# Layer-norm tiles and matmuls interleaved, longer leads, and W2 in pieces: a transformer layer on eight cores

## The chip, the cores and the metric

The kernel runs on all 8 NeuronCores of one Trainium2 chip. Every core gets 2 of the 16 sequences and all the weights, and the cores exchange nothing. The metric is the time of one execution on the device, in microseconds (us), taken from the slowest core. Engines in the rows: PE is TensorE (PEld its weight loads), DVE is VectorE, ACT is ScalarE, POOL is GpSimd, SP is SyncE, which here only issues transfers; SPq and POOLq are the issuing queues.

## What is computed

For each sequence of 2048 tokens and width 1024, one pre-norm layer with 16 heads of 64:

```python
x = x + proj(softmax(q k^T / 8) v)      # q, k, v = layernorm(x) @ w_qkv + b_qkv
h = round_to_1/256(layernorm(x) @ w1 + b1)          # 1024 -> 4096
g = round_to_1/256(piecewise_linear_gelu(h))        # 33 points on [-4, 4]
x = x + round_to_1/256(g @ w2 + b2)                 # 4096 -> 1024
```

x, the weights and the output are float32 in memory; the matmuls run in bf16 with sums in float32.

## The kernel before

The program writes the instruction stream of every engine by hand. `Queue.do` appends an instruction to an engine's list with the semaphore values it waits for, and each engine runs its list strictly in order; a wait therefore holds everything behind it on that engine. `sy` is SP's queue and `gp` POOL's queue of transfers; `gp` transfers can change float32 to bf16 on the way. A `Ring` hands out buffer slots in turn, and a slot carries the waits that make it free. Filler work is written as generators that yield after each matmul. A `Lane(lo, hi, tasks)` spreads the declared number of yields evenly over steps `lo` to `hi`. `at(dt, fn)` runs `fn` at the `tick()` that comes dt steps later.

**First stage** (L736 to L757). x of sequence 0 comes in 16 tiles of 128 tokens into 7 slots (3 in `xin`, 4 in `xext`). In groups of four: statistics of four tiles on DVE (`ln_stats`), square root on ACT (`ln_rstd_sqrt`), then per tile an apply on ACT (`ln_apply`) and 8 transposes on PE with a copy to `xn` on ACT (`transposes`). After the group come the matmuls of the group before: four V tiles (`v_task`, L472, evicted on DVE L483) and one tile each of K and Q (`qk_tile`, L404, evicted on ACT L410), which share the two banks of `pF` with the transposes.

**Attention.** 16 head pairs g (8 for each sequence) of PAIR = 32 steps, 512 steps in all. A step issues the scores of two key tiles (L630, L633) into the two banks of `pS`, an exp for each on ACT (L638), some filler, and the PV matmuls (L650, into `pO`) of the step before. Eight steps make one block of 512 queries; then `emit_tail` copies the sums and values out of `pO` (L667), sends the denominators through memory to spread them over the partitions (`dena`, `dn`), takes reciprocals (L676), sends them back and broadcasts them (`denb`, `rb`), and multiplies (L685, L687); the four parts run 1, 3, 4 and 6 steps after the copy. The filler is the Q and K of later pairs (`qk_task`, with the guard: the largest squared norms give an upper bound for the exp, `guard_norm` and `guard`), V of the other heads, layer norm of sequence 1 (`ln1_task`, written to `xnd` and loaded again by `load_xn` at step 6 x 32), the weight loads (`load_wqk`), the output projection of sequence 0 (`proj_task`, L566, L570, L573) and layer norm of FFN block 0 (`ln2_task`). `ffn_loads` starts the loads of W1 (five slots) and of W2 (four transfers) over buffers that attention has finished with.

**FFN.** 8 blocks of 512 tokens with 16 steps k each. A step has two halves of W1 (8 matmuls each, L863), each evicted with rounding on ACT (L870), the split of the rounded number on DVE (L874, L876), two gelus at neighbouring points on ACT (L881, L883; `gelu_step`), and the interpolation on DVE (L890 to L892) with the cast to `gbuf` (L894; `act_step`). W2 matmuls (`w2_half`, L915) follow 17 steps later. In block 0 their place is taken by `proj_task` of sequence 1, one matmul after each W1 matmul, in the two banks of `pO`. Each step ends with `gelu_step(k - 1)` and `act_step(k - 1)`.

Of the kernel before, what the change touches and what calls it, by code (L numbers as in the profile page):

```python
# [19 lines left out]
NTT = 16  # L20
# [109 lines left out]
def build():  # L130
# [24 lines left out]
    with es:  # L155
# [52 lines left out]
        wpj = sb("wpj", [128, NDC, D], BF16, esA)  # L208
        vt = [vt0, vt1]
# [78 lines left out]
        s_xl = [sem(f"s_xl{i}") for i in range(7)]  # L288
        s_xs = [sem(f"s_xs{i}") for i in range(3)]
        xslot = [xin[:, i, :] for i in range(3)] + [xext[:, i, :] for i in range(4)]  # L290
        xring = Ring(range(7))
# [157 lines left out]
        def qk_task(g):  # L449
            gt = []  # L450
            for which in (1, 0):
                for tb in range(4):
                    yield from qk_tile(g, which, tb, ve)
                if which == 0 and g + 2 < NG:
                    load_wqk(g + 2)
                yield
                yield
                gt.append(guard_norm(which))
                yield
                yield  # L460
            yield
            guard(g, gt)
            yield
# [64 lines left out]
        def load_xn():  # L528
            for tb in range(4):

                t = sy.dma([stg_tok[14], stg_tok[15], qkv_last[0]], s_xn[tb], lambda e, tb=tb: e.dma_start(
                    out=xn[:, :, tb * 512:(tb + 1) * 512], in_=xnd[tb]))
                for i in range(4):
                    xn_tok[(1, 4 * tb + i)] = t
# [8 lines left out]
        def proj_task(s, tts, ring, bank, bring):  # L543

            got = {}

            def load(tt):
                if tt not in tts:
                    return
                i, fr = plring.take()  # L550
                tl = sy.dma([*fr, *[att_store[(s * NPAIR + p, tt // 4)] for p in range(NPAIR)]], s_pl[i],
                            lambda e: e.dma_start(out=pl[:, i, :, :], in_=attd[s, tt]))
                got[tt] = (i, tl, *x_load(x[s, tt * 128:(tt + 1) * 128, :], ring))

            load(tts[0])
            yield
            load(tts[0] + 1)
            yield
            for tt in tts:
                row = tt * 128  # L560
                i, tl, k, tx = got.pop(tt)
# [19 lines left out]
                load(tt + 2)  # L581
# [77 lines left out]
        def emit_tail(g, qb, t_pv):  # L659
# [34 lines left out]
            at(1, step1)  # L694
            at(3, step2)
            at(4, step3)
            at(6, step4)
# [20 lines left out]
        def first_matmuls(gi):  # L718
            yield from v_task(0, 0, range(4 * gi, 4 * gi + 4))
            for which in (1, 0):  # L720
                yield from qk_tile(0, which, gi, sc)

# [6 lines left out]
        for tt in range(7):  # L729
            first_load(tt)  # L730
        for gi in range(4):
            sl = slice(4 * gi, 4 * gi + 4)
            ks = [x_got[tt] for tt in range(4 * gi, 4 * gi + 4)]
            for i, (k, tok) in enumerate(ks):
                t = ln_stats(k, lnst[:, 4 * gi + i, :], [tok])
            t = ln_rstd_sqrt(lnst[:, sl, :], lnr[:, sl, :], [t])  # L736
            late = None
            for i in range(5):
                if i < 4:
                    tt = 4 * gi + i  # L740
                    row = ln_apply(ks[i][0], lnr[:, tt, :], [t, ks[i][1]], sc, xring)
                    first_load(tt + 7)
                if late is not None:
                    tt = 4 * gi + i - 1
# [268 lines left out]
```

How the kernel before makes its waits and increments, by code:

```python
    def run(self, e):  # L79
        for ws, fn, sem, by in self.items:
            for s, v in ws:
                e.wait_ge(s, v)
            if fn is not None:
                ins = fn(e)
                if sem is not None:
                    ins.then_inc(sem, by)
```

## Time and profile before

| what | value |
|---|---|
| median of 3 runs | 2583.2 us (2570.23 to 2589.48) |
| profiled execution | 2585.74 us |
| its slowest core (5), first to last instruction | 2584.2 us |
| its fastest core (2) | 2555.4 us |
| PE busy on core 5 | 2292.8 us, 89% |
| ACT busy | 1586.0 us, 61% |
| DVE busy | 1357.3 us, 53% |
| chain that ended last | PE 68%, DMA 8%, ACT 8%, DVE 8%, issue 7% |

The busy shares are means over stages with different limits. The 1024 exps on ACT (1111 ns each) belong to attention alone; the 2048 W1 and 2048 W2 matmuls belong to the FFN. The granted clock is TensorE's clock as a share of its full speed. A wait for several semaphores is put down to the one that came last by the profile.

### The profile page before, as it was taken

How to read it: one execution, taken by the hardware profiler on the slowest of the kernel's cores; microseconds unless marked ns; L12 is line 12 of the kernel's file. 1: busy time of each engine (PE TensorE's matmuls, PEld its weight loads, DVE VectorE, ACT ScalarE, POOL GpSimd, SP SyncE). 2: the span in 40 equal slices, each digit the busy share in tenths (PEclk: the TensorE clock that was granted, in tenths of full speed). 3: DMA queues.
4: the chain of work that ended last, by engine and by line, in shares of the span. 5: the costliest groups of instructions: out<-in, count | busy, mean ns of one | idle time of the engine just before them, and what ended most of it. 6: DMA issues, size and time to landing. Idle time of an engine off the chain costs nothing.

```text
span 2584.2 us, 33191 instructions; the slowest of 8 cores (2555.4 to 2584.2 us)
## 1 busy us (share of the span) xinstructions
PE 2292.8 (89%) x10896; PEld 938.0 (36%) x10896; DVE 1357.3 (53%) x2180; ACT 1586.0 (61%) x1611; POOL 68.8 (3%) x82
## 2 busy tenths in 40 slices
PE   3689898999799999999779857789999999999998
PEld 1333333333233333333223322234444444444443
DVE  3234444433123333333234547676888888888883
ACT  3378787778688888888658722234555555555440
POOL 0100000001000000000000000000000000000000
PEclk9799999999899999999889978778999999999999
DMA  6161443333512321120584434443334343433322
GB/s 162 23 109 37 80 85 49 76 56 61 86 38 40 44 37 30 31 38 23 105 177 129 138 134 159 135 154 112 123 123 148 117 135 119 154 123 125 124 90 74
DMA packets 224182, 245.76 MB, mean 95 GB/s; under 512 B 144720, under 2 KB 152912, under 8 KB 224016
## 3 DMA queue, kind: packets, MB, share of 16 engines
q1 hardware_dynamic: 147536, 211.07, 26.4%
q0 software_dynamic: 76480, 32.57, 10.8%
q8 instruction: 93, 1.52, 0.3%
q14 instruction: 73, 0.60, 0.1%
HBM read 228.42 MB, written 55.05 MB: 110 GB/s over the span
## 4 chain that ended last, share of the span: by engine, by line
PE 68%; DMA 8%; ACT 8%; DVE 8%; issue 7%; SPq 1%; DVEq 0%; ACTq 0%; POOL 0%; POOLq 0%
PE pO L915 17%; PE pS L863 17%; PE pO L650 12%; PE pS L630 8%; PE pF L404 7%; ACT PT L638 6%; PE pF L472 4%; DMA rb<-denb 2%; DVE ue L667 2%; PE pO L566 2%; DMA denb<-dn 1%; PE pF L566 1%; PE pF L355 1%; DMA dena<-ue 1%; DVE nf L892 1%
## 5 line engine op out<-in xcount | busy, mean ns | idle before, releaser
L638 ACT ACTIVATE PT<-pS,gb 128x1024 bf16<-128x1024 f32 x1024 | 1082.3, 1111 | 292.1 <-PE pS L633 286.7
L863 PE MATMUL pS<-xn,w1s 128*128 128x512 bf16 x2048 | 801.7, 393 | 0.0
L915 PE MATMUL pO<-w2b,gbuf 128*128 128x512 bf16 x2048 | 740.7, 383 | 3.0 <-DVE gbuf L894 3.0
L650 PE MATMUL pO<-PT,vt 128*65 128x512 bf16 x2048 | 539.1, 387 | 36.0 <-DVE ue L667 35.5
L870 ACT ACTIVATE n<-pS,b1t 128x512 int16<-128x512 f32 x256 | 175.4, 686 | 551.0 <-PE pS L863 531.2
L630 PE MATMUL pS<-qp,kp 64*128 64x512 bf16 x1024 | 356.3, 386 | 41.8 <-ACT PT L638 38.7
L633 PE MATMUL pS<-qp,kp 64*128 64x512 bf16 x1024 | 360.4, 390 | 0.0
L650 PEld LDWEIGHTS pO<-PT,vt 128*65 128x65 bf16 x2048 | 224.6, 113 | 270.1 <-issue 80.6
L863 PEld LDWEIGHTS pS<-xn,w1s 128*128 128x128 bf16 x2048 | 205.8, 100 | 253.4 <-issue 50.5
L915 PEld LDWEIGHTS pO<-w2b,gbuf 128*128 128x128 bf16 x2048 | 202.0, 99 | 247.5 <-issue 26.7
L404 PE MATMUL pF<-xn,wqk 128*128 128x512 bf16 x1024 | 275.0, 384 | 11.1 <-DMA wqk<-wqkv 11.0
L630 PEld LDWEIGHTS pS<-qp,kp 64*128 64x128 bf16 x1024 | 85.0, 93 | 336.3 <-issue 329.8
L890 DVE TENSOR_TENSOR g<-g 128x1024 f32<-128x1024 f32 x128 | 156.4, 1222 | 57.0 <-ACT g L883 57.0
L566 PE MATMUL pO<-wpj,pl 128*128 128x512 bf16 x256 | 116.4, 455 | 72.3 <-DVE xin L570 51.7
L892 DVE SCALAR_TENSOR_TENSOR nf<-g 128x1024 int16<-128x1024 f32 x128 | 156.8, 1225 | 13.3
L891 DVE TENSOR_TENSOR g<-g,n 128x1024 f32<-128x1024 f32 x128 | 156.8, 1225 | 13.3
L472 PE MATMUL pF<-wv,xn 128*128 128x512 bf16 x512 | 140.3, 400 | 19.9 <-DVE vt L483 14.4
L883 ACT ACTIVATE g<-nf,c 128x1024 f32<-128x1024 int16 x128 | 145.4, 1136 | 0.0
L667 DVE COPY ue<-pO 65x512 f32<-65x512 f32 x128 | 82.0, 680 | 116.7 <-PE pO L650 116.6
L483 DVE TENSOR_TENSOR vt<-pF,bvbc 128x512 bf16<-128x512 f32 x64 | 44.3, 692 | 182.4 <-PE pF L472 182.4
L881 ACT ACTIVATE g<-nf 128x1024 f32<-128x1024 int16 x128 | 134.1, 1048 | 0.0
L404 PEld LDWEIGHTS pF<-xn,wqk 128*128 128x128 bf16 x1024 | 77.8, 98 | 147.0 <-issue 93.5
(82 smaller groups left out, 1303.1 us busy)
## 6 DMA issues: line engine op xcount, KB each, us to landing
w1s<-w1d SPq DMA_DIRECT2D x256, 256.0 KB, 2.7
xin<-x1s SPq DMA_DIRECT2D x64, 512.0 KB, 4.3
xin<-x SPq DMA_DIRECT2D x47, 512.0 KB, 4.7
rb<-denb SPq DMA_DIRECT2D x64, 256.0 KB, 3.6
x1s<-xin SPq DMA_DIRECT2D x32, 512.0 KB, 3.3
out<-xin SPq DMA_DIRECT2D x32, 512.0 KB, 3.0
xext<-x SPq DMA_DIRECT2D x17, 512.0 KB, 6.1
wqk<-wqkv POOLq DMA_DIRECT2D x32, 256.0 KB, 6.5
```

Of the source, the lines that this page charges most:

```text
L404: t = pe.do([*fr, wqk_tok[g], *need], lambda e, dc=dc: e.matmul(pF[:, f, :], wqk[:, k, which, dc, :], xn[:, dc, cols], start=(dc == 0), st ...
L472: t = pe.do([*fr, wv_tok[(s, nb)], xn_tok[(s, tt)]], lambda e, dc=dc, f=f, tt=tt: e.matmul(pF[:, f, :], xn[:, dc, tt * 128:(tt + 1) * 128] ...
L566: t = pe.do([*fr, tl, t_later], lambda e, dc=dc, f=f, i=i, cols=cols: e.matmul(bank[:, f, :], pl[:, i, dc, :], wpj[:, dc, cols], start=(dc ...
L630: pe.do(need, lambda e, kt=kt, sl=sl: e.matmul(pS[:, sl, 0:512], kp[0:64, r, kt * 128:(kt + 1) * 128], qp[0:64, r, qb * QB:(qb + 1) * QB], ...
L633: t = pe.do([], lambda e, kt=kt, sl=sl: e.matmul(pS[:, sl, 512:1024], kp[64:128, r, kt * 128:(kt + 1) * 128], qp[64:128, r, qb * QB:(qb + ...
L638: t = sc.do([t, gb_tok[g], pfree[pl_]], lambda e, sl=sl, pl_=pl_: e.activation(PT[:, pl_, :], pS[:, sl, :], AF.Exp, bias=gb[:, g:g + 1], s ...
L650: t = pe.do(need, lambda e, kt=kt, pl_=pl_, i=i: e.matmul(pO[0:65, i, :], vt[nb][:, kt, (h + i) * 65:(h + i + 1) * 65], PT[:, pl_, i * 512 ...
L863: lambda e, dc=dc, h=h, wk=wk: e.matmul(pS[:, sl, h * 512:(h + 1) * 512], w1s[:, wk, dc, :], xn2[:, b % 2, dc, :], start=(dc == 0), stop=( ...
L870: nt_ = sc.do([t, m_tok.get(k - 3), t_b1, t_att_ve], lambda e, h=h, hm=hm: e.activation(n16[:, nb3, h * 512:(h + 1) * 512], pS[:, sl, h * ...
L891: t = ve.do([t, u_tok[k]], lambda e: e.tensor_tensor(g1[:, i, :], g1[:, i, :], n16[:, nb3, :], ALU.mult))
L892: t = ve.do([t], lambda e: e.scalar_tensor_tensor(nf[:, i, :], g0[:, i, :], 256.0, g1[:, i, :], ALU.mult, ALU.add))
L915: lambda e, hm=hm: e.matmul(pO[:, f, :], gbuf[b % 2][:, hm, tt * 128:(tt + 1) * 128], w2b[:, hm, cols], start=(hm == 0), stop=(hm == NHM - ...
```

## The change

- **First stage.** An eighth slot for x (`xmore`). Per tile: V matmuls of the tile four back, then the transposes of this tile, with the apply of the next one ahead of them. The statistics, the square root and the first apply of the next group stand ahead of the K and Q tiles of the group before. `load_wqk(1)` stands ahead of the wait for the last x tile.
- **Guard.** `guard_norm` runs 3 steps after its four tiles and `guard` 7 steps after, by `at`, instead of after two and one empty yields. A `qk_task` is declared with 64 units instead of 72. `load_wqk(g + 2)` comes after the last tile as before.
- **Denominators.** The four parts run 2, 4, 5 and 9 steps after the copy.
- **load_xn.** Four loads on POOL's queue, each after the last Q tile that reads its part, instead of four together on SP's queue.
- **Projection.** Loads three tiles ahead instead of two, the first three by `proj_ahead`: for sequence 0 before the last `qk_task`, for sequence 1 directly behind attention. No leading yields in `proj_task`.
- **Order of the lane from step 256.** `qk_task(9)` to `(12)` each before its V part. The lanes' ends move by a few steps. Layer norm of FFN blocks 0 and 1 both run from step 456 to 510.
- **W2.** 32 transfers of 128 rows instead of 4 of 1024 rows, one at each third step, the rest two at a time in FFN block 0. W1's first loads start 8 steps after `ffn_start`.
- **End of attention.** The 8 ticks behind the last step, in which the last denominators are finished, become two in each of the FFN steps 0 to 4; b2 is loaded at step 5.
- **FFN.** `gelu_step(k - 1)` is issued between the two halves of W1 of step k, and `act_step(k - 1)` ahead of the split (L874, L876) of step k.

```diff
-        xslot = [xin[:, i, :] for i in range(3)] + [xext[:, i, :] for i in range(4)]
-        xring = Ring(range(7))
+        xslot = [xin[:, i, :] for i in range(3)] + [xmore[:]] + [xext[:, i, :] for i in range(4)]
+        xring = Ring(range(8))
...
                 for tb in range(4):
                     yield from qk_tile(g, which, tb, ve)
-                if which == 0 and g + 2 < NG:
-                    load_wqk(g + 2)
-                yield
-                yield
-                gt.append(guard_norm(which))
-                yield
-                yield
-            yield
-            guard(g, gt)
-            yield
+                    if which == 0 and g == NPAIR - 1:
+                        load_xn(tb)
+                at(3, lambda which=which: gt.append(guard_norm(which)))
+            if g + 2 < NG:
+                load_wqk(g + 2)
+            at(7, lambda: guard(g, gt))
...
+        def load_xn(tb):
+            t = gp.dma([stg_tok[4 * tb + 2], stg_tok[4 * tb + 3], qkv_last[0]], s_xn[tb], lambda e: e.dma_start(
+                out=xn[:, :, tb * 512:(tb + 1) * 512], in_=xnd[tb]))
...
+        def proj_load(s, tt, ring):
+            i, fr = plring.take()
+            tl = sy.dma([*fr, *[att_store[(s * NPAIR + p, tt // 4)] for p in range(NPAIR)]], s_pl[i],
+                        lambda e: e.dma_start(out=pl[:, i, :, :], in_=attd[s, tt]))
+            proj_got[(s, tt)] = (i, tl, *x_load(x[s, tt * 128:(tt + 1) * 128, :], ring))
...
-                load(tt + 2)
+                if tt + ahead < NTT:
+                    proj_load(s, tt + ahead, ring)
...
-            at(1, step1)
-            at(3, step2)
-            at(4, step3)
-            at(6, step4)
+            at(2, step1)
+            at(4, step2)
+            at(5, step3)
+            at(9, step4)
...
+        t = first_stats(0)
+        row = first_apply(0, t)
+        for gi in range(5):
+            for i in range(4):
+                tt = 4 * gi + i
+                if gi > 0:
+                    all_of(v_task(0, 0, (tt - 4,)))
+                if gi < 4:
+                    late, row = row, None
+                    if i < 3:
+                        row = first_apply(tt + 1, t)
                     xn_tok[(0, tt)] = transposes(late, xn[:, :, tt * 128:(tt + 1) * 128], [], sc)
-                late = row
+            if gi < 3:
+                t = first_stats(gi + 1)
+                row = first_apply(4 * gi + 4, t)
             if gi > 0:
-                for _ in first_matmuls(gi - 1):
-                    pass
-        for _ in first_matmuls(3):
-            pass
+                all_of(qk_tile(0, 1, gi - 1, sc))
+                all_of(qk_tile(0, 0, gi - 1, sc))
         guard(0, [guard_norm(1), guard_norm(0)])
-        t_x0 = xn_tok[(0, NTT - 1)]
-        gp.wait([t_x0])
         load_wqk(1)
+        gp.wait([xn_tok[(0, NTT - 1)]])
         load_wqk(2)
...
-            for c in range(4):
-                t = gp.dma(w_over, s_w2, lambda e, c=c: e.dma_start(
-                    out=w2b[:, 8 * c:8 * c + 8, :],
-                    in_=w2[c * 1024:(c + 1) * 1024, :].rearrange("(c q) n -> q c n", q=128)))
-            w2_tok.append(t)
-            yield
+
+        def load_w2():
+            c = len(w2_tok)
+            if c < NHM:
+                w2_tok.append(gp.dma(w_over, s_w2, lambda e: e.dma_start(
+                    out=w2b[:, c, :], in_=w2[c * 128:(c + 1) * 128, :])))
...
-            Lane(6 * PAIR + 5, 8 * PAIR, [(v_task(1, 0, range(16)), 128), (qk_task(8), 72)]),
+            Lane(6 * PAIR + 3, 8 * PAIR - 8, [(v_task(1, 0, range(16)), 128), (qk_task(8), 64)]),
...
-            if n == NG * PAIR - 12:
-                lanes.append(Lane(n, NG * PAIR, [(ln2_task(0, ve, xring), 12)]))
+            if n == 14 * PAIR + 8:
+                lanes.append(Lane(n, NG * PAIR - 2, [(ln2_task(0, ve, xring), 12), (ln2_task(1, ve, xring), 12)]))
+            if w_over and n % 3 == 0:
+                load_w2()
...
         emit_pv(*prev)
-        for _ in range(8):
-            tick()
+        for _ in proj_ahead(1, 3, xring):
+            pass
...
+                if h == 0 and k > 0:
+                    gelu_step(k - 1)
             n_tok[k] = nt_
+            if k > 0:
+                act_step(k - 1)
...
+            if k < NHP:
+                load_w2()
+                load_w2()
+            if k < 5:
+                for _ in range(2):
+                    tick()
+            if k == 5:
+                t_gbuf.extend(att_store[(NG - 1, qb)] for qb in range(NQB))
+                load_b2()
```

## Rows read from the trace of the kernel before

**Rows 1.** Spans and mean granted clock of cores 2 and 5.

```profile
core 2: 2555.4 us, clock 0.960
...
core 5: 2584.2 us, clock 0.948
```

**Rows 2.** Windows: length, busy us PE, PEld, DVE, ACT, POOL, clock, DMA share, GB/s.

```profile
900.00:1250.00 350.00, 334.16 (x1650) 124.67 (x1649) 119.50 (x218) 303.27 (x287) 11.43 (x13) 1.00 0.19 32
...
1522.00:1722.00 200.00, 147.14 (x544) 58.61 (x545) 137.54 (x207) 55.18 (x65) 0.00 (x0) 0.80 0.45 148
1722.00:1806.00 84.00, 84.00 (x333) 35.42 (x332) 61.72 (x92) 38.97 (x46) 0.00 (x0) 0.81 0.40 129
1806.00:2500.00 694.00, 694.00 (x3347) 319.94 (x3345) 572.61 (x786) 354.28 (x417) 0.00 (x0) 1.00 0.40 127
```

**Rows 3.** Chain that ended last, first stage: start us, us, what.

```profile
53.50 0.69 DVE bst L306
...
60.65 1.25 ACT xntm L341
62.03 1.01 PE pF L355 x8
...
68.79 8.25 PE pF L472 x32
...
96.71 7.95 PE pF L472 x32
...
108.11 6.92 PE pF L472 x32
...
117.30 16.59 DMA wqk<-wqkv
```

**Rows 4.** Timeline, POOL: issue of the first V weights.

```profile
3.94 0.93 POOL L283 DMA_DIRECT2D wv<-wqkv  x1
```

**Rows 5.** Transfers issued from 0 to 40 us: count, KB, median us to landing.

```profile
wv<-wqkv POOLq DMA_DIRECT2D x1, 1024.0 KB, 23.8
```

**Rows 6.** TensorE's waits, 140 to 1502 us: total us, times, longest us.

```profile
PE pO L650 <- DVE ue L667: 35.5, 31, 7.1
PE pF L566 <- DMA pl<-attd: 20.4, 2, 14.9
PE pF L472 <- DVE vt L483: 14.4, 1, 14.4
PE pF L443 <- DVE gmb L441: 6.8, 7, 1.5
PE pF L472 <- DVE stg L363: 5.5, 1, 5.5
PE pF L566 <- DVE xin L570: 5.2, 2, 4.6
PE pF L426 <- DVE sq L419: 5.2, 5, 1.4
```

**Rows 7.** VectorE's waits for transfers, 140 to 1502 us.

```profile
DVE att L685 <- DMA rb<-denb: 103.0, 30, 14.2
DVE dn L676 <- DMA dn<-dena: 77.8, 25, 22.4
```

**Rows 8.** Transfer queues, 1262 to 1345 us: packets, MB, share of 16 engines.

```profile
q0 software_dynamic: 4160, 8.39, 63.6%
```

**Rows 9.** TensorE's waits, 1522 to 1722 us.

```profile
PE pO L566 <- DVE xin L570: 51.7, 14, 5.4
PE pO L566 <- DVE nt L322: 19.6, 1, 19.6
```

**Rows 10.** Chain that ended last, one step of FFN block 0.

```profile
1553.56 1.24 DVE g L890
...
1554.89 1.24 DVE g L891
...
1557.89 0.69 DVE xin L570
```

More of the change, by code:

```diff
@@ L541, in build, with proj_ahead, proj_task @@
         st_tok = {}
[L543 to L555, printed above, removed]
-            yield
-            load(tts[0] + 1)
-            yield
-            for tt in tts:
+        proj_got = {}
+        def proj_load(s, tt, ring):
[3 more added lines that the diff above has]
+            proj_got[(s, tt)] = (i, tl, *x_load(x[s, tt * 128:(tt + 1) * 128, :], ring))
+        def proj_ahead(s, n, ring):
+            for tt in range(n):
+                proj_load(s, tt, ring)
+                yield
+        def proj_task(s, ahead, ring, bank, bring):
+            for tt in range(NTT):
                 row = tt * 128
-                i, tl, k, tx = got.pop(tt)
+                i, tl, k, tx = proj_got.pop((s, tt))
                 for nb in range(2):
@@ L716, in cast_w1 @@
                 in_=w1[:, hm * 128:(hm + 1) * 128].rearrange("(c q) n -> q c n", q=128)))
[L718 to L721, printed above, removed]
         x_got = {}
@@ L727, in first_load, with first_stats @@
                 x_got[tt] = x_load(x[0, tt * 128:(tt + 1) * 128, :], xring)
-        for tt in range(7):
-            first_load(tt)
[L731 to L744, printed above, removed]
+        def first_stats(gi):
+            sl = slice(4 * gi, 4 * gi + 4)
+            for i in range(4):
+                k, tok = x_got[4 * gi + i]
+                t = ln_stats(k, lnst[:, 4 * gi + i, :], [tok])
+            return ln_rstd_sqrt(lnst[:, sl, :], lnr[:, sl, :], [t])
@@ new lines, in build, with first_apply, all_of @@
+        for tt in range(8):
+            first_load(tt)
+        def first_apply(tt, t):
+            row = ln_apply(x_got[tt][0], lnr[:, tt, :], [t, x_got[tt][1]], sc, xring)
+            first_load(tt + 8)
+            return row
+        def all_of(gen):
+            for _ in gen:
+                pass
+        t = first_stats(0)
+        row = first_apply(0, t)
+        for gi in range(5):
+            for i in range(4):
+                tt = 4 * gi + i
[5 more added lines that the diff above has]
+                        row = first_apply(tt + 1, t)
@@ L827, in build @@
         emit_pv(*prev)
-        for _ in range(8):
-            tick()
-        t_att_pe = pe_last()
-        t_att_ve = (ve.sem, ve.sem.n)
+        for _ in proj_ahead(1, 3, xring):
+            pass
         t_att_sc = (sc.sem, sc.sem.n)
-        t_att_st = [att_store[(NG - 1, qb)] for qb in range(NQB)]
         s_b2 = sem("s_b2")
@@ L935, in build @@
         lring, pring = Ring([]), Ring([])
-        lring.free = xring.free[:1]
-        pring.free = xring.free[1:]
-        t_proj = [None, None]
-        proj1 = Lane(0, NHP * 16, [(proj_task(1, range(16), pring, pO, oring), 258)])
-        lanes = [Lane(0, NHP, [(ln2_task(1, sc, lring), 12)])]
+        t_gbuf = []
+        proj1 = Lane(0, NHP * 16, [(proj_task(1, 3, xring, pO, oring), 256)])
+        lanes = []
         for k in range(NST + 18):
@@ L959, in build @@
             if k == NHP - 1:
-                t_proj[1] = pe_last()
-            if 1 <= k <= NST:
+                t_gbuf.append(pe_last())
+                keep = [(i, toks) for i, toks in xring.free if i < 3]
+                t_gbuf.extend(t for i, toks in xring.free if i == 3 for t in toks)
+                lring.free, pring.free = keep[:1], keep[1:]
+            if k == NST:
                 gelu_step(k - 1)
```

64 lines of the change are left out of this document (32 added, 32 removed).

## The prediction, made before the change was built or run

> **What bounds the kernel now.** I read the spans of the cores first, then windows of the slowest core, then within each stage the waits of the engine that sets its pace. Core 5 is the slowest at 2584.2 us, core 2 the fastest at 2555.4 [rows 1]. The profiled run took 2585.7 us, 1.5 us more than that span, and the median of the three runs is 2583.2 us, 2.5 us less. So the sum is made on core 5's span and 1.5 us is added at the end.
>
> The span has five stages: the first layer norm with its matmuls, 0 to about 140 us; attention, to 1502 us; a hole, to 1522 us; feed-forward (FFN) block 0 with the second projection woven in, to 1722 us; and the other seven blocks. In the last stage TensorE is busy without a break, 694.00 of 694.00 us at granted clock 1.00 with 3347 matmuls [rows 2]; only a better clock could shorten it. In attention a stretch with few disturbances, 900 to 1250 us, gives 287 exps in 350 us, 1.22 us per exp and 2.44 us per step of two. All 1024 exps at that pace are 1249 us, so the stage's 1362 us hold 113 us of stalls. In block 0 TensorE is busy 147 of 200 us at a granted clock of 0.80. The gain must come from the first stage, the stalls, the hole and block 0, and the change touches all four.
>
> **First stage.** It is a cycle of 27.9 us per group of four tiles: the long runs of V matmuls begin at 68.79 and 96.71 us [rows 3]. In one cycle VectorE reaches the next group's statistics (53.50) only behind the evictions, the apply is at 60.65, then four transposes, and only then the matmuls; TensorE idles meanwhile. The change puts a V tile between two transposes, and the statistics ahead of the Q and K tiles. From the end of a group's fourth V tile the new cycle is: eviction 0.9 us, statistics to apply 7.15 us (53.50 to 60.65), apply 1.25, the K eviction behind it on ScalarE 0.7, some 0.5 of hand-overs: 10.5 us. Then four V tiles of 1.73 us (6.92/4, warm) with three transposes of 1.01 us between them, 10 us, and 2 us more because TensorE idled about 6 us and its clock falls. That is 22.5 us instead of 27.9. The first V tile can't start before its weights land at about 28 us: issued at 3.94 us [rows 4], 23.8 us on the way [rows 5]. The eighth x tile has a slot of its own now, so that the second group's apply isn't behind that. My schedule: the V tiles of group 0 end at 42 us, of group 1 at 64.5, of group 2 at 87. Group 3 has no statistics behind it, so the rest follows at once, to about 99 us. Before, it ends at 115.03 (108.11 + 6.92). The next weights are issued behind that last V tile in both, and their 16.59 us stay exposed; issuing the next pair's ahead of the wait for the last x tile changes nothing, since that wait is long passed. Gain 16 us; bounds 8 (half-level clock for most of it) and 26 (half of the 10.5 us hidden too).
>
> **Attention.** What the change aims at are TensorE's waits other than for a free score bank; the seven of [rows 6] sum to 93.0 us.
> - Denominators: 35.5 us for the copy that empties the PV bank, 5.5 us behind a staging copy. The cause is VectorE in order: it waited 103.0 us in 30 places for the broadcast reciprocals (longest 14.2) and 77.8 us in 25 for the sums [rows 7]. The steps go from 1, 3, 4, 6 to 2, 4, 5, 9. The broadcast gets 4 steps (9.8 us) instead of 2 (4.9), and the multiply now stands behind the next copy, which is 8 steps away; a wait of 4.9 us goes whole, and what is left of a longer one falls where two filler banks give slack. On SP's queue each step is only later, never ahead of more than the projection's loads. I take off 36 of 41.
> - Second sequence's normalized x: the 14.4 us wait is VectorE stuck for sums (22.4 us, its longest) that were behind four 1 MB loads on SP's queue. They move to POOL's queue, one behind each Q tile, 8 matmuls apart. Behind them there are only the next pair's weights and casts. I take off 13.
> - W2: four transfers at once, while the projection waits 20.4 us for its loads and 5.2 us for an eviction. The 8.39 MB that POOL's queue wrote took 63.6% of 83 us [rows 8], 53 us of all engines; 32 pieces are 1.65 us each, one per 3 steps (7.3 us), so a quarter of the engines. 23 pieces come before attention ends and 9 in block 0. With three loads ahead I take off 23. Bad bound: each of the 23 pieces delays a denominator by its 1.65 us, 38 us.
> - Guard: 12.0 us for squares, sums and bias, chained hand-overs to VectorE. With leads of 3 and 7 steps nothing waits, and the instructions are the same: 10.
> - Refill: the stalls are 20 us more than these waits, mostly the clock and pipeline after long ones. I take a third, 7. Task counts of 64 instead of 72 move the same matmuls: nothing. Their cover is ScalarE's loop; without it they would cost what the last tasks lose, 8 empty steps of 0.1 us. Block 1's layer norm moves in: four transposes and copies, minus 2.
>
> Sum 36 + 13 + 23 + 10 + 7 - 2 = 87 us. Bounds 45 (the pieces' 38 us lost) and 105.
>
> **The hole.** TensorE waits 19.6 us [rows 9]. The row names a VectorE line, but what came last were the projection's loads, which SP issued behind the whole chain of the last denominators and the b2 load. Now three loads stand right behind the last copy: 1.3 us of copies and about 4 us of transfer. 5.5 us stay, gain 14; bounds 8 and 16.
>
> **Block 0.** Its 16 steps take 12.5 us each (200/16). TensorE waits 51.7 us in 14 places for a projection eviction [rows 9]. That eviction stands behind the gelu arithmetic on VectorE, 1553.56 to 1557.89 [rows 10], which waits for two gelus, which wait on ScalarE for the second W1 half of the same step: TensorE waits for work that hangs on its own last matmul. The change issues the gelus of step k-1 after the first half and the arithmetic before the new rounding, and drops two leading yields, so that the eviction isn't pushed behind a step. Then VectorE is the bound: 137.54 us busy in this stage [rows 2], less some 6 for block 1's layer norm, is 8.2 us per step; 13 instructions (207/16) with 0.09 us between them (1553.56 + 1.24 to 1554.89) add 1.2; with the last denominators, b2 and waits at either end I take 10. TensorE's 32 matmuls are 6.6 us at 3347 in 694 us and 13.3 at the half level; with one cold spell per pause 8.5, under VectorE. 16 x 10 = 160, gain 40. Bounds 5 (half level most of the time) and 50.
>
> **Blocks 1 to 7.** The new order of gelu and rounding has TensorE as cover, busy without a break: 0. From 1722 to 1806 us the granted clock is 0.81 and 333 matmuls take 84 us, against 69 at the later pace: 15 us that may come or go on any core, so I keep them; they are a bound of the range.
>
> Sum: 16 + 87 + 14 + 40 = 157. 2584.2 - 157 = 2427, plus 1.5 is 2429; the forecast is **2430 us**.
>
> **A rule against it.** On core 5 the granted clock is 0.81 for 84 us and then 1.00 for 694 us, both with TensorE always busy [rows 2]. The Trainium skill ("TensorE: Matmul & The Clock Gate", Part 1) says that a peak-current limiter holds a die at 13/16 of the clock once three of its cores run dense matmuls, and to budget for that. By that rule the whole dense stretch would be at 0.81; the trace agrees for 84 us and disagrees for 694.
>
> **Rivals.** (A) The stages behave as said, 2395 to 2460: 0.60. (B) Attention gives half, because pieces and moved loads replace the burst by many small waits: for it, each denominator passes four transfers; against it, the engines' load of a quarter. 2430 + 43 = 2473: 0.17. (C) Block 0 stays at 12 us a step by another hand-over or a cold TensorE: for it, the clock of 0.80 there; against it, that the loop is cut. 2430 + 32 = 2462: 0.12. (D) B and C together, about 2505: 0.04. (E) The change doesn't do what it says: the waits covered each other and each removed one shows the next, 2560 to 2605: 0.04. (F) The other side: a denser kernel holds the clock at 0.81 through attention and FFN. A dense microsecond then costs 0.22 more (84 against 69). FFN: 694 x 0.22 = 153. Attention: TensorE is busy 334 of 350 us [rows 2], 2.33 us of each 2.44 us step, which becomes 2.84: 512 x 0.40 = 205. 2430 + 358 = 2788 at the worst; it makes the kernel slower by over 1% from (157 + 26)/0.22 = 830 dense us at 0.81: 0.03.
>
> A measurement can tell about 1% here, 26 us. A to D are faster by more, 0.93; E is within, 0.04; F slower, 0.03. The range 2385 to 2490 holds A, B and C with most of their bounds, about 0.85.
>
> **What would show it.** Right: V matmul runs every 22 us at the start and the first exps 16 us earlier; VectorE's waits for rb under 30 us; no TensorE wait over 5 us for pl, the PV copy or vt; no hole over 8 us; block 0 steps of 10 us with VectorE over 85% busy. Wrong: waits in the rhythm of the W2 pieces, block 0 steps of 12 us or more with the clock at 0.5 to 0.7, or an FFN at 0.81.

## The result, and the profile after

The changed kernel takes 2480.0 to 2491.4 us, 0.963 of the time before (interval 0.958 to 0.968): 96 us less (82 to 110), where 153 were forecast and the range began at 93. In some executions of either kernel the cores of one die or of both run at a lower granted clock (2758 and 2674 us of this one, 2690 of before), and the comparisons of times here leave them out, so the median over all its runs, 2579 us, is not used; the profile of the version with the old leads, below, is of such an execution. The profiled run took 2480.0 us, the shortest of the four; its slowest core is 1, where before it was core 5 [rows 1].

Spans and mean granted clock of cores 1 and 6, the slowest and the fastest:

```profile
core 1: 2478.4 us, clock 0.977
...
core 6: 2453.5 us, clock 0.980
```

I cut both slowest cores at the same events: the exps running steadily, the last PV matmul, the start and the end of FFN block 0.

| stage | before | after | difference | forecast |
|---|---|---|---|---|
| first stage | 136.5 | 124.4 | -12 | -16 |
| attention | 1366.1 | 1309.3 | -57 | -87 |
| hole | 19.7 | 5.1 | -15 | -14 |
| block 0 | 199.4 | 162.4 | -37 | -40 |
| the rest | 862.5 | 877.2 | +15 | 0 |
| sum | 2584.2 | 2478.4 | -106 | -157 |

The means over all eight cores differ by -14, -58, -15, -39 and +20 us, so the two cores stand for the others. The sum is 106 and not 96 because of the two executions that were profiled: 2585.7 us is above the median before, and 2480.0 is the shortest after.

So three stages did about what was said, attention gave two thirds, and the FFN loop, costed at nothing, got slower. Before, four cores had a stretch at clock 0.81 in the rest, as core 5 in [rows 2], and took 862 to 865 us for it, and the other four, without one, 850. So the stretch cost 13 us (the prediction has 15). After, all eight cores take 876 to 878 us without such a stretch: like for like the loop lost 27.

Windows of core 1 after (length, busy us PE, PEld, DVE, ACT, POOL, clock, DMA share, GB/s), to be laid beside [rows 2]:

```profile
900.00:1250.00 350.00, 320.96 (x1578) 121.20 (x1576) 119.65 (x220) 287.91 (x272) 24.02 (x40) 0.98 0.27 55
...
1204.00:1304.00 100.00, 67.18 (x300) 23.69 (x300) 35.31 (x74) 55.21 (x53) 16.96 (x32) 0.85 0.86 187
1439.00:1601.00 162.00, 125.05 (x508) 51.46 (x507) 134.56 (x199) 53.35 (x62) 0.00 (x0) 0.90 0.57 180
1750.00:2300.00 550.00, 541.10 (x2612) 248.16 (x2610) 439.38 (x611) 271.52 (x326) 0.00 (x0) 1.00 0.39 128
```

The second line is the first surprise: 53 exps in 100 us, 1.9 us each instead of 1.22, and POOL, which issued W2 in 4 transfers before, issues 32 here. The third is the forecast of block 0 come true: VectorE 134.56 of 162 us, 83%, with TensorE's clock up from 0.80 to 0.90. The fourth is the second surprise: the dense FFN isn't dense. TensorE has 9 us of gaps in 550, at clock 1.00.

Waits of TensorE, then of VectorE, from 120 to 1430 us (us in total, times, longest):

```profile
PE pF L444 <- DVE gmb L442: 17.5, 8, 8.5
PE pO L645 <- DVE ue L662: 16.4, 21, 6.7
PE pF L560 <- DVE xin L564: 16.2, 2, 12.6
PE pF L405 <- DMA wqk<-wqkv: 10.6, 1, 10.6
PE pF L560 <- DVE xmore L564: 6.7, 1, 6.7
```

```profile
DVE dn L671 <- DMA dn<-dena: 68.6, 12, 22.1
...
DVE att L680 <- DMA rb<-denb: 29.0, 4, 11.4
```

Beside [rows 6] and [rows 7]: the PV copy (ue) fell from 35.5 to 16.4 us, the loads of pl are gone, the waits for rb fell from 30 places to 4. But the guard (gmb) rose from 6.8 to 17.5, the projection's evictions hold TensorE for 22.9 us, and VectorE's longest wait for dn is still 22 us.

**Where the W2 pieces went.** POOL's queue, then VectorE's and TensorE's rows behind it (start, us, engine, line, operation, idle before and its releaser):

```profile
1213.96 16.96 POOL L788 DMA_DIRECT2D w2b<-w  x32 [119.80 <-PE pS L628]
```

```profile
1247.15 0.20 DVE L671 RECIPROCAL dn<-dn 128x8 f32<-128x8 f32 x1 [22.14 <-DMA dn<-dena]
...
1266.57 0.68 DVE L680 TENSOR_TENSOR att<-ue,rb 64x512 bf16<-64x512 f32 x1 [11.38 <-DMA rb<-denb]
...
1285.17 0.20 DVE L671 RECIPROCAL dn<-dn 128x8 f32<-128x8 f32 x1 [12.54 <-DMA dn<-dena]
```

```profile
1248.09 0.58 PE L560 MATMUL pF<-wpj,pl 128*128 128x512 bf16 x1 [12.58 <-DVE xin L564]
...
1268.83 1.01 PE L560 MATMUL pF<-wpj,pl 128*128 128x512 bf16 x2 [6.69 <-DVE xmore L564]
```

All 32 pieces left in 17 us. `load_w2` is called at each third step of the program, but a step of the program is a place in the lists, not a time. The pieces' own waits (`w_over`) are met together, and nothing else in POOL's list holds one back until TensorE has got to its step. The pieces then take a median of 31.4 us to land, a 4 KB hop of the denominators (dena to dn) takes 8.8 us in the median of three from 1214 to 1300 us, after 2.0 in the median of 40 from 300 to 1100, and VectorE stands 22, 11 and 13 us for the hops.

**The FFN loop.** VectorE, then ScalarE, in one step of it, 2000 to 2008 us:

```profile
2000.02 0.43 DVE L906 CAST gbuf<-nf 128x1024 bf16<-128x1024 int16 x1
2000.36 0.42 DVE L886 TENSOR_SCALAR nf<-n 128x1024 int16<-128x1024 int16 x1
2000.88 0.43 DVE L888 TENSOR_SCALAR n<-n 128x1024 int16<-128x1024 int16 x1
2003.07 1.23 DVE L902 TENSOR_TENSOR g<-g 128x1024 f32<-128x1024 f32 x1 [1.76 <-ACT g L895]
...
2007.05 0.43 DVE L906 CAST gbuf<-nf 128x1024 bf16<-128x1024 int16 x1
2007.40 0.42 DVE L886 TENSOR_SCALAR nf<-n 128x1024 int16<-128x1024 int16 x1
```

```profile
2000.87 1.06 ACT L893 ACTIVATE g<-nf 128x1024 f32<-128x1024 int16 x1 [3.79 <-DVE nf L886]
2001.83 1.13 ACT L895 ACTIVATE g<-nf,c 128x1024 f32<-128x1024 int16 x1
```

The chain closes on itself: the split (L886) of this step releases the gelus, these the interpolation (L902 to L906), and behind that, because `act_step(k - 1)` now stands ahead of the split, comes the next split. From 2000.36 to 2007.40 that is 7.04 us, step after step. In the old order the split isn't behind the interpolation of the step before, and the step is TensorE's: 6.91 us in most steps before.

**Granted clock.** It is 1.00 over the 550 us above, and 0.99 or 1.00 on each of the eight cores, all of them in the FFN, so rival F did not happen in this execution. By the Trainium skill ("TensorE: Matmul & The Clock Gate", Part 1), which says the peak-current limiter holds a die at 13/16 once three cores run dense matmuls, it should be 0.81; the row disagrees with it.

### The profile page after: what moved, and what is told of

Its sections match the earlier page's. It is cut to its first block, busy times and chain, and to the rows that moved or that the text cites. A ratio compares the mean times of both kernels' runs of the same rounds, so it can differ in the third digit from the quotient of the medians.

```text
span 2478.4 us, 32994 instructions; the slowest of 8 cores (2453.5 to 2478.4 us)
## 1 busy us (share of the span) xinstructions
PE 2242.0 (90%) x10896; PEld 927.4 (37%) x10896; DVE 1346.5 (54%) x2184; ACT 1575.7 (64%) x1607; POOL 85.9 (3%) x114
## 4 chain that ended last, share of the span: by engine, by line
PE 50%; DVE 19%; issue 12%; DMA 9%; ACT 9%; SPq 1%; DVEq 1%; ACTq 0%; POOL 0%; POOLq 0%
PE pO L645 11%; PE pO L927 9%; PE pS L625 8%; PE pS L871 7%; ACT PT L633 7%; PE pF L405 6%; PE pF L469 4%; DVE nf L904 3%; DVE g L903 3%; DVE g L902 3%; DMA w1s<-w1d 3%; DMA dn<-dena 2%; ACT g L895 2%; PE pF L560 1%; DMA wv<-wqkv 1%
## 5 line engine op out<-in xcount | busy, mean ns | idle before, releaser
L871 PE MATMUL pS<-xn,w1s 128*128 128x512 bf16 x2048 | 782.1, 383 | 17.6 <-DMA w1s<-w1d 13.5
L645 PE MATMUL pO<-PT,vt 128*65 128x512 bf16 x2048 | 530.1, 381 | 17.2 <-DVE ue L662 16.4
L878 ACT ACTIVATE n<-pS,b1t 128x512 int16<-128x512 f32 x256 | 164.9, 674 | 112.7 <-PE pS L871 109.5
L902 DVE TENSOR_TENSOR g<-g 128x1024 f32<-128x1024 f32 x128 | 156.5, 1222 | 101.4 <-ACT g L895 101.1
L560 PE MATMUL pO<-wpj,pl 128*128 128x512 bf16 x256 | 105.0, 410 | 41.9 <-DVE xin L564 30.5
L414 DVE TENSOR_SCALAR kp<-pF,bqt 128x512 bf16<-128x512 f32 x60 | 45.0, 749 | 156.9 <-PE pF L405 156.6
```

Source lines behind the costliest of these rows:

```text
L645: t = pe.do(need, lambda e, kt=kt, pl_=pl_, i=i: e.matmul(pO[0:65, i, :], vt[nb][:, kt, (h + i) * 65:(h + i + 1) * 65], PT[:, pl_, i * 512 ...
L871: lambda e, dc=dc, h=h, wk=wk: e.matmul(pS[:, sl, h * 512:(h + 1) * 512], w1s[:, wk, dc, :], xn2[:, b % 2, dc, :], start=(dc == 0), stop=( ...
L902: t = ve.do([gel_tok[k]], lambda e: e.tensor_tensor(g1[:, i, :], g1[:, i, :], g0[:, i, :], ALU.subtract))
```

## Experiments

All ratios are to the kernel before, and "the kernel after" is at 2480 to 2491 us. Most undo or mend one part of it alone; where one builds on another, it says so. Where no interval stands, the two or three times given are all that there is. "Mean of the cores" is the length of a stage, averaged over the eight cores of the profiled execution. Where attention is left as it is in the kernel after, that mean still differs between executions, from 1303 to 1311 us in four of them.

**The W2 pieces held back.** Each piece also waits for the last matmul issued so far:

```diff
-                w2_tok.append(gp.dma(w_over, s_w2, lambda e: e.dma_start(
+                w2_tok.append(gp.dma([*w_over, pe_last()], s_w2, lambda e: e.dma_start(
```

> The changed kernel, and each W2 piece also waits for the matmul that stands before it in TensorE's program. Theory P (burst): in the changed kernel all 32 pieces left POOL's queue in 17 us (1214 to 1231 us), because nothing on that queue held them back; they kept all DMA engines busy for 80 us, and TensorE waited 33 us between 1221 and 1317 us. Paced by waits the pieces go out one per three steps, the denominators' waits of 22, 11 and 12.5 us go, and attention is 25 to 35 us shorter: about 2455 us, ratio to the kernel before 0.950. Rival Q (bytes): W2 costs the same whenever it is moved beside the projection's loads, the waits are spread instead of removed: within 8 us of the changed kernel, about 2484 us.

2446.9 to 2455.3 us, ratio 0.951 (0.948 to 0.955): 32 us less. POOL's queue, and the window of the burst again:

```profile
1227.49 0.54 POOL L788 DMA_DIRECT2D w2b<-w  x1 [8.48 <-PE pS L628]
1234.55 0.53 POOL L788 DMA_DIRECT2D w2b<-w  x1 [6.51 <-PE pS L628]
1242.02 0.53 POOL L788 DMA_DIRECT2D w2b<-w  x1 [6.94 <-PE pS L628]
```

```profile
1204.00:1304.00 100.00, 90.15 (x441) 34.58 (x447) 50.75 (x100) 80.38 (x76) 5.88 (x11) 0.98 0.69 182
```

Now a piece leaves every 7 to 8 us, about as the forecast had it, and the same 100 us hold 76 exps instead of 53. From 1204 to 1404 us VectorE's longest wait for dn is 6.9 us instead of 22. The stall was the burst.

**The old order of gelu, split and interpolation in all of the FFN.**

```diff
-                if h == 0 and k > 0:
-                    gelu_step(k - 1)
...
-            if k > 0:
-                act_step(k - 1)
...
-            if k == NST:
+            if 1 <= k <= NST:
```

> The changed kernel with the FFN's old order: both gelus of step k-1 behind both evictions of step k, the interpolation behind the split. Theory L (loop): with the interpolation ahead of the split, a split waits for the interpolation before it, the gelu waits for the split and the next interpolation for the gelu: 2.2 + 4.3 + 0.5 = 7.04 us per step against 6.83 us for TensorE, 24 us over the seven later blocks. So blocks 1 to 7 get back to 6.83 us a step, 15 to 28 us shorter, while block 0 goes from about 10 to 12 or 13 us a step, 35 to 45 us longer: 10 to 25 us above the changed kernel, 2495 to 2510 us. Rival S (SP's queue): the later blocks lose because W1's loads stand behind output stores; that comes from the same order, so here it expects the same. Rival N: the order does nothing in the later blocks and what differs there is the granted clock; then this kernel is 35 to 45 us above the changed one.

2504.1 to 2511.2 us, ratio 0.973 (0.969 to 0.978): 25 us more than the kernel after. In the mean of the cores block 0 takes 212 us instead of 160, and the rest 850 instead of 877: block 0 wants the new order by more than the loop dislikes it. TensorE's step is 6.91 us there as before, and not 6.83 as the expectation has it.

**The new order in block 0 only** (`if h == 0 and 0 < k <= NHP`, the same for `act_step`, and the old place from there on).

> The changed kernel with its new FFN order in steps 0 to 16 alone and the old order from step 17 on. Theory L (loop): keeps block 0 at 10 us a step and takes the later blocks from 7.04 to 6.83 us: 15 to 28 us below the changed kernel, 2457 to 2470 us. Rival N (granted clock): within 5 us of the changed kernel.

2455.6 to 2462.1 us, ratio 0.954 (0.949 to 0.959): 24 us less than the kernel after. Its slowest core in the FFN:

```profile
1750.00:2300.00 550.00, 550.00 (x2662) 253.71 (x2661) 455.33 (x627) 283.47 (x334) 0.00 (x0) 1.00 0.41 131
```

TensorE is busy 550 of 550 us, with 2662 matmuls where the kernel after has 2612. The rest takes 850 us in the mean of the cores, 27 less than in the kernel after, as in the kernel before where its clock stays up. Between gelus the mean step is 7.00 us here and 7.18 after (over some 108 steps, the longer ones at block ends among them); 112 steps by 0.18 are 20 of these 27 us. TensorE's last wait, for gbuf, is 3.0 us instead of 6.0; the other 4 us are not told apart.

**The output's stores moved from SP's to POOL's queue**, with semaphores of their own, since TensorE's longest list of waits in the loop was for W1 (16 waits, 13.5 us), whose loads stand behind those stores.

> The changed kernel with the output stores on POOL's queue, with semaphores of their own, so that no W1 load stands behind a store that waits for VectorE. Rival S (SP's queue makes the later FFN blocks slow) expects 6.83 us a step there, no TensorE wait for W1 (13.5 us before) and 15 to 25 us below the changed kernel, 2460 to 2470 us. Theory L (the loop of gelu, interpolation and split) expects the waits for W1 to go, others to take their place, the step to stay at 7.04 us and the time within 5 us of the changed kernel, about 2484 us.

2482.5 and 2488.0 us: no change. Its waits for W1 are gone, others stand in their place (8.0 us for ScalarE's eviction, 6.5 for the layer norm's copy) and the step is still 7.04 us, with TensorE busy as before (539.04 us of 550, against 541.10). The W1 waits were slack inside the closed chain, not its cause.

**The old leads of the denominators** (1, 3, 4, 6 steps in place of 2, 4, 5, 9).

> The changed kernel with the denominators' four parts again 1, 3, 4 and 6 steps after the copy. By the prediction the longer leads took 36 us out of TensorE's waits, of which the kernel before had 41 us behind VectorE: expected are waits of VectorE for rb of 80 to 100 us in all again, TensorE's wait for the PV copy back at 30 us or more, and 20 to 36 us more than the changed kernel, 2505 to 2520 us. The rival, that the leads matter little once the big transfers are moved, expects within 8 us of it.

2498.3 and 2503.5 us, ratio 0.971 (0.967 to 0.975): 16 us more than the kernel after by the times, 22 by the ratios, whose intervals just touch. That is between what the two sides expected. On core 4 VectorE waits for rb in 36 places again, 114.4 us in all, where the kernel after has 4, and TensorE waits 29.2 us for the PV copy, against 16.4.

**Both cures**, pieces held back and the new order in block 0 only.

> The changed kernel with both cures: W2's pieces wait for TensorE's program, and the new FFN order holds in steps 0 to 16 only. If burst and loop are separate causes, the two gains add: 31 + 24 us below the changed kernel, about 2430 us, ratio 0.942, which is the forecast's sum. If they share something (the same transfers late, the same clock), less than 45 us of the 55 arrive: 2440 us or more.

2421.3 and 2425.5 us, ratio 0.941 (0.938 to 0.945). By the ratios 30 and 24 us were won alone and 56 are won together: the two losses lie in different stages.

**And the guard in two parts.** In `guard`, the sum on VectorE and the matmul that reads it were issued back to back, so TensorE's list ran into a sum that stood behind whatever VectorE was stuck on.

```diff
-            at(7, lambda: guard(g, gt))
+            sums = []
+            at(5, lambda: sums.append(guard_add(gt)))
+            at(8, lambda: guard_rest(g, sums[0]))
```

> The kernel with both cures, and the guard in two parts: the sum on VectorE 5 steps after the Q tiles, the matmul that needs it 8 steps after, instead of both 7 steps after. Theory G: TensorE's waits for that sum (15 to 27 us in 9 or 10 places in the changed kernel and its variants, up to 11.9 us at once, against 6.8 us in the kernel before) come from issuing the sum and the matmul back to back, with VectorE held by a late transfer in between: they go, and the time is 8 to 20 us below the kernel with both cures. Rival: VectorE is late anyway and the next thing in TensorE's order waits instead; within 5 us.

2411.7 to 2418.4 us, ratio 0.938 (0.936 to 0.940): 8 us less. The two intervals overlap, but attention is 10 us shorter in the mean of the cores, and the waits for gmb, 16.5 us on the slowest core of the version before, are gone.

**Seven x tiles at the start instead of eight**, on top of that, to see why the V weights came late.

> The kernel with both cures and the split guard, and only seven x tiles loaded at the start; the eighth follows behind the first apply, into the free eighth slot. Theory X: in the changed kernel the eighth tile's 512 KB stands among the first transfers beside the V weights, which took 31.1 us instead of 23.8 and were waited for 9.3 us (35.19 us instead of 28): the V weights land at about 28 to 30 us again, the first stage ends 3 to 6 us earlier, and the time is that much below the kernel without this edit. Rival: the second group's statistics now wait for the eighth tile (28.8 us in the kernel before) and give it back; within 2 us.

2416.3 and 2423.0 us, and the V weights still take 30.9 us on core 0, 29.5 in the mean of the cores, as in the version without this edit. But the edit changes nothing on the chip. The eighth load is only called later in the program: its slot is free, it waits for nothing, and SP's queue issues it with the others. Eight loads are out by 4.9 us:

```profile
1.07 1.34 SPq L296 DMA_DIRECT2D xin<-x  x3
2.46 0.43 SPq L296 DMA_DIRECT2D xmore<-x  x1
2.93 1.99 SPq L296 DMA_DIRECT2D xext<-x  x4
```

So this measures the version before a second time and says nothing of the eighth tile.

**The casts of W1 spread too.** `cast_w1`, which the change doesn't touch, issues transfers with no wait of their own, and six of them leave together. The timeline of all engines of the kernel after, cut to POOL and what waited behind it:

```profile
598.35 5.24 POOL L709 DMA_DIRECT2D w1d<-w  x6
...
609.60 0.68 DVE L680 TENSOR_TENSOR att<-ue,rb 64x512 bf16<-64x512 f32 x1 [8.09 <-DMA rb<-denb]
...
620.96 0.20 DVE L671 RECIPROCAL dn<-dn 128x8 f32<-128x8 f32 x1 [9.26 <-DMA dn<-dena]
...
622.80 2.12 ACT L633 ACTIVATE PT<-pS,gb 128x1024 bf16<-128x1024 f32 x2 [9.97 <-PE pS L628]
```

Now, on top of the guard in two parts, one cast at the steps 2, 12 and 22 of a pair, each waiting for the last matmul issued:

```diff
-            w1d_tok[0] = gp.dma([], s_wd,
+            w1d_tok[0] = gp.dma([pe_last()], s_wd,
...
-            if m == 0 and 1 <= g <= 11:
-                for hm in range(3 * g - 3, min(3 * g, NHM)):
-                    cast_w1(hm)
+            if m in (2, 12, 22) and 1 <= g <= 11 and 3 * g - 3 + m // 10 < NHM:
+                cast_w1(3 * g - 3 + m // 10)
```

> The kernel with both cures and the split guard, and W1's casts issued singly, 10 steps apart, each behind the matmul that stands before it in TensorE's program. Theory C: casts have no wait and go out as soon as POOL's queue reaches them, six at once behind the four moved x loads at 598 us; ScalarE's longest gap in undisturbed attention, 7 to 10 us at 623 to 626 us, and the 3 to 5 us ones near 350 and 430 us are from such bursts. They go, 8 to 15 us below the kernel without this edit. Rival: the bursts' bytes are spread and each pair loses a little; within 4 us.

2402.5 to 2411.8 us, on top of the version before the seven tiles (median 2404.8 against 2415.0): 10 us less, and the gap of 10 us near 623 is gone. The ranges just touch, and attention in the mean of the cores is 1259 us, after 1262 and 1267 in the two profiled executions without the edit, so the gain is 3 to 10 us, not surely more than the rival's 4. The idle time ahead of the exps in gaps over 1.5 us is 38 us in all of attention, after 85 in the kernel after and 134 before.

**load_xn back on SP's queue**, alone, in the kernel after.

> The changed kernel with the four loads of the second sequence's normalized x together on SP's queue at step 192 again. By the prediction the move to POOL's queue took 13 us off TensorE's waits: expected are a wait of VectorE for the sums of about 20 us near 640 us and 8 to 15 us more than the changed kernel, 2493 to 2500 us. The rival, that with longer leads for the denominators the place of these loads doesn't matter, expects within 5 us of 2484 us.

2492.5 and 2496.5 us: 10 us more, and in the mean of the cores attention is 15 us longer. The four loads, and VectorE behind them:

```profile
599.03 9.25 SPq L524 DMA_DIRECT2D xn<-xnd  x4
```

```profile
633.41 0.20 DVE L669 RECIPROCAL dn<-dn 128x8 f32<-128x8 f32 x1 [25.83 <-DMA dn<-dena]
```

TensorE's wait behind it is for gmb, 18.0 us, so the guard's fault has a part in it.

**Only block 0's order, in the kernel before** (and no leading yields in `proj_task`).

> The kernel before with nothing but the new order of gelu and interpolation in FFN steps 0 to 16 and the projection without its two leading yields. The forecast's term for block 0 alone: its steps go from 12.5 to 10 us, 30 to 42 us below the kernel before, ratio 0.984 to 0.988. If that gain needs the other parts (the third load ahead, block 1's layer norm moved out), less than 20 us arrive, ratio above 0.992.

2535.4 to 2543.6 us, beside one execution of the kernel before at 2574.0 on the same chip: 33 us less. In the mean of the cores block 0 takes 156 us instead of 200, 43 less, and attention 1371 instead of 1362, little more than executions differ by; whether the missing yields of the first projection cost that was not run. The hole is untouched in it: its longest wait for pl is 20.0 us.

**b2 multiplied later.** Block 0 after has one step of 18.3 us, behind this row of VectorE:

```profile
1497.72 0.69 DVE L849 TENSOR_SCALAR b2bc<-b2bc 128x1024 f32<-128x1024 f32 x1 [6.13 <-DMA b2bc<-b]
```

Everything so far but the seven tiles, with b2 loaded at step 5 and multiplied by 256 at step 8:

> All the cures together: the W2 pieces and the W1 casts paced by TensorE, the new order of gelu and split only in FFN block 0, the guard in two parts, and b2 multiplied by 256 at step 8 instead of right behind its transfer at step 5 (in the kernel after, VectorE waits 6.1 us there and one step of block 0 takes 18.3 us where the others take 10). Theory: that step becomes 10 to 12 us, the version with the paced casts at 2402 to 2412 us goes down by 5 to 8, to about 2400. Rival: the step is late for another reason (the last denominators' ticks end there too), less than 2 us, about 2405.

2398.3 to 2403.7 us (median 2400.3), ratio 0.933 (0.929 to 0.936). That step is 9.6 us long, where the version with the casts had 15.3. The whole differs by less than the runs do, but block 0 is 155.3 us in the mean of the cores, after 159.7: 4.4 us less. Its TensorE in the FFN is dense again:

```profile
1700.00:2250.00 550.00, 550.00 (x2663) 254.00 (x2661) 453.66 (x625) 282.94 (x333) 0.00 (x0) 1.00 0.41 130
```

**x tiles 8 to 15 behind the V weights**, on top of that.

```diff
-                x_got[tt] = x_load(x[0, tt * 128:(tt + 1) * 128, :], xring)
+                x_got[tt] = x_load(x[0, tt * 128:(tt + 1) * 128, :], xring, [wv_tok[(0, 0)]] if tt >= 8 else ())
```

> The same, but x tiles 8 to 15 are issued only once the V weights have landed. Over the eight cores the V weights took 22.7 to 29.5 us in the kernel before (mean 26.1) and 28.0 to 32.0 in the kernel after (mean 30.0), with the transfer engines full from 5 to 43 us. Theory Y, the second round of x tiles shares the engines with them: mean of the cores 27 us or less, first V matmuls before 32 us, the second group's statistics 2 to 5 us later, the whole within 3 us of the version without it. Theory Z, the first round of eight tiles and the small transfers set it: still 29 to 31 us, and the whole 3 to 8 us slower because the x tiles come later for nothing.

The V weights of the kernel after (core 1) and of this one (core 0), KB and us from issue to landing:

```profile
wv<-wqkv POOLq DMA_DIRECT2D x1, 1024.0 KB, 31.1
```

```profile
wv<-wqkv POOLq DMA_DIRECT2D x1, 1024.0 KB, 24.3
```

Over the eight cores they took 22.5 to 25.7 us, mean 24.0, against 27.3 to 31.2, mean 29.1, in the version without the hold. So theory Y holds: the second round of x shares the transfer engines with them. The second group's statistics, expected later, start at the same 18.6 us, and the third group's at 40.9 instead of 46.1, both in the mean of the cores. The Trainium skill ("DMA: Bandwidth & Descriptors", Queues, rings and completion order) has each engine go round the queues that have work, a packet at a time; the two rows agree with that, x on one queue and the weights on another. The last K and Q matmuls of the stage start at 96.11 us instead of 100.87, the first stage is 4 us shorter in the mean of the cores, and the whole takes 2395.6 to 2403.2 us (median 2397.7, ratio 0.932, interval 0.928 to 0.935): 3 us less, which the intervals don't tell from nothing.

## Why the prediction was right or wrong, step by step

**First stage: -12 of -16.** TensorE after:

```profile
35.19 3.57 PE L469 MATMUL pF<-wv,xn 128*128 128x512 bf16 x8 [9.27 <-DMA wv<-wqkv]
...
45.95 1.89 PE L469 MATMUL pF<-wv,xn 128*128 128x512 bf16 x8 [0.50 <-DVE vt L480]
...
48.89 3.61 PE L405 MATMUL pF<-xn,wqk 128*128 128x512 bf16 x16 [0.61 <-DVE vt L480]
57.66 2.94 PE L469 MATMUL pF<-wv,xn 128*128 128x512 bf16 x7 [5.16 <-ACT kp L411]
...
79.34 3.57 PE L469 MATMUL pF<-wv,xn 128*128 128x512 bf16 x8 [5.26 <-ACT kp L411]
```

The new cycle is 21.7 us (57.66 to 79.34), with 22.5 forecast: the mechanism and its size were right. What failed is the start, "the first V tile can't start before its weights land at about 28 us": they landed at 35. The 23.8 us were those of one core; over eight cores before they were 22.7 to 29.5 (mean 25.9), and after 28.0 to 32.0 (mean 30.0). With the second round of x held back they were 24.0 in the mean. That round leaves at the same 20 us before and after, so sharing with it is shown, but not why it costs 4 us more after; there 10 to 12 x tiles land ahead of the weights, before 7 to 10. The eighth tile of the first round doesn't do it alone, since it is there at 24.0 us too; what it does together with the second round no run has tested. Group 0's V tiles ended at 47.8 instead of 42, and all later groups kept 4 to 6 us of that.

**Attention: -57 of -87.** Term by term:

- *W2, forecast 23.* The step that failed is the pace, "32 pieces are 1.65 us each, one per 3 steps (7.3 us)". The 1.65 us were taken from [rows 8] and the 7.3 us from where the call stands in the program. The change issues them in 17 us; holding them back is worth 32 us. Even my bad bound, 38 us for the denominators, assumed the pace and only doubted what a piece costs. The trace of before could have told it: its four transfers left together too, within 3.5 us, and so did six casts.
- *Denominators, forecast 36.* The copy's waits fell by 19 us (35.5 to 16.4) and undoing the leads costs 16 to 22. I let the whole wait go, "a wait of 4.9 us goes whole". Two things stay. VectorE still waits up to 22 us behind bursts of transfers, and a lead of 5 us shortens such a stall without ending it. And small waits stay without any burst: with both cures the copy still costs TensorE 13.6 us in 21 places, none over 2.5. The term was mis-sized by about half.
- *xn, forecast 13*: undoing it costs 10, 15 in attention itself. Right in place and size.
- *Guard, forecast 10*: "with leads of 3 and 7 steps nothing waits" failed. Waits for gmb rose from 6.8 to 17.5 us, because the lead lies ahead of the pair of sum and matmul and not between them. I had counted the steps from the tiles and not looked at what `guard` issues as one. Splitting it is worth 8.
- *Layer norm of block 1 and refill*: not told apart.

Undoing the leads and the moved loads gives back 26 to 32 of the 57 us. What the others come from no run shows. In the mean of the cores 44 of 58 us are won before step 256, where neither W2 nor the third load ahead plays a part; the 64 units for a `qk_task`, which I put at nothing, are untested there. Attention is 1362 us before and 1260 with all the cures, 102 less and more than the forecast 87: the stalls were there to be had, and in part by other edits than those that I priced.

**The hole: -15 of -14.** TensorE waits 4.98 us for pl, forecast 5.5:

```profile
1438.85 0.59 PE L560 MATMUL pO<-wpj,pl 128*128 128x512 bf16 x1 [4.98 <-DMA pl<-attd]
```

**Block 0: -37 of -40.** Most steps take 9.0 to 10.5 us with VectorE 83% busy, and the order alone, in the kernel before, takes 43 us off block 0 and 33 off the whole. The one step held for b2 (8 us over the others) is more than what is missing; multiplying it later gave 4.4 us. My 10 us a step left room for "waits at either end", but the b2 wait is in the middle, where `load_b2` and its multiply stand back to back, the guard's fault again.

**Blocks 1 to 7: +15 (27 like for like) of 0.** After attention's 30 us this is the largest error. "The new order of gelu and rounding has TensorE as cover" was argued from TensorE's busy share. TensorE's step was a bound, and I hadn't closed the other loop, over ScalarE and VectorE: gelu to gelu over VectorE by the new order is 0.51 (split, 2000.36 to 2000.87), 2.20 (gelus, to 2003.07) and 4.33 (interpolation and cast, to 2007.40), 7.04 us, against TensorE's 6.91. The interpolation's 4.33 us stand in [rows 10] too (1553.56 to 1557.89), and the two gelus' 1136 and 1048 ns in the page of the profile before, so the new order could have been seen to be no shorter than TensorE's step. The 6.6 us that I took for 32 matmuls, from 3347 in 694 us, are too low, since shorter transposes are counted with them.

```profile
L883 ACT ACTIVATE g<-nf,c 128x1024 f32<-128x1024 int16 x128 | 145.4, 1136 | 0.0
...
L881 ACT ACTIVATE g<-nf 128x1024 f32<-128x1024 int16 x128 | 134.1, 1048 | 0.0
```

**Rivals.** B (attention gives less because pieces and moved loads make waits) was nearest: 2473 against 2480 to 2491. That is partly luck: attention gave 57 us and not half of 87, its waits came in one lump and not in many small ones, and the loop, which nothing in my list had, took back the difference. C, E and F did not occur in the executions compared. The direction and the chance of 0.93 for it held; the range, ending at 2490, held the times only near its edge, and the longest of the four, 2491.4, is outside. Of the signs named for being right, the V runs every 22 us, the waits for rb (29.0 us), for pl and for vt and the short hole came; the first exps were 11.5 us earlier and not 16, the PV copy still held TensorE for 6.7 us at once, and VectorE was busy for 83% of block 0 and not 85%.

## What to carry to other kernels

A call at step n of a program that writes queues ahead of time is a place, not a time: a transfer is paced only by a wait on something that itself runs at that pace, and one whose waits are long met leaves at once, with all its fellows (the W2 pieces, the casts, the eighth x tile). Before an order of two engines' work is changed in a loop that a third engine bounds, close the loop through the two, instruction by instruction, and compare its length with the bound; 2% of cover is soon gone. A lead counts only between producer and consumer, so an `at` that issues both gives none.

## What was not expected of the hardware

A transfer of 4 KB took 8.8 us in the median of three, and one chain of them held VectorE for 22 us, while 32 pieces of 256 KB were on their way on the other queue; from 300 to 1100 us it took 2.0. The same 1 MB load of weights at the start differs between cores of one execution by up to 6.8 us (22.7 and 29.5 us before), which a forecast from one core's row doesn't see.
